# Weighing key rows by attention probabilities in three float32r passes, in a decoder layer on one Trainium2 core

## The reference

```python
q = l @ Wq                                  # l: normed latents (x after the first layer norm)
kv_in = jnp.concatenate([x, l], axis=1)     # normed context and latents: the 128 "key rows" of a batch
k, v = jnp.split(kv_in @ Wkv, 2, axis=-1)
w = jnp.einsum('bhqd,bhkd->bhqk', q * scale, k * scale)
w = jax.nn.softmax(w, axis=-1)
out = jnp.einsum('bhqk,bhkd->bhqd', w, v)
return out.transpose(0, 2, 1, 3).reshape(B, S_lat, INNER) @ Wo
```

## Time and profile before

| | us |
|---|---|
| median of three runs | 1594.77 |
| lowest, highest of them | 1588.36, 1599.34 |
| the profiled execution | 1598.73 |
| its span from first to last instruction | 1596.9 |
| TensorE busy in the span | 1421.5 (89%) |
| VectorE, ScalarE, GpSimd busy | 1102.3, 1033.0, 901.6 |

### The profile page before, as it was taken

One profiled execution on the slowest core, in us unless ns is written; L12 is line 12 of the kernel. 1 busy time (PEld: TensorE's weight loads), 2 busy tenths in 40 slices (PEclk: granted clock), 3 DMA queues, 4 the chain that ended last, 5 costly groups with the idle time before them and its releaser, 6 DMA issues. The chain is left out here.

```text
span 1596.9 us, 36673 instructions
## 1 busy us (share of the span) xinstructions
PE 1421.5 (89%) x10509; PEld 1235.3 (77%) x10509; DVE 1102.3 (69%) x4106; ACT 1033.0 (65%) x3829; POOL 901.6 (56%) x1233
## 2 busy tenths in 40 slices
PE   6799999999999999999999999999995688889940
PEld 4688888888878888888888888888884688889940
DVE  4466677776677777777767777677656577777765
ACT  3577777777777777776777767777762455555535
POOL 4355665666666666566665566656544255545555
PEclk8899999999999999999999999999998899999975
DMA  3000000000000000000000000000001776667746
GB/s 88 11 11 10 16 15 15 17 18 14 17 15 16 18 15 16 15 16 18 15 16 15 17 15 18 16 15 8 10 10 42 222 221 211 216 200 231 206 140 203
DMA packets 64625, 96.19 MB, mean 60 GB/s; under 512 B 10892, under 2 KB 48786, under 8 KB 64306
## 3 DMA queue, kind: packets, MB, share of 16 engines
q1 hardware_dynamic: 44738, 71.90, 15.1%
q0 software_dynamic: 8896, 16.94, 3.1%
q10 hardware_dynamic: 10800, 5.06, 1.2%
HBM read 71.55 MB, written 23.35 MB: 59 GB/s over the span
## 5 line engine op out<-in xcount | busy, mean ns | idle before, releaser
L696 ACT ACTIVATE probs<-ps_s,neg_max 128x128 f32<-128x128 f32 x1024 | 361.7, 366 | 291.2 <-DVE neg_max L929 291.2
L511 POOL TENSOR_TENSOR probs_n<-probs,inv_sum 128x512 f32<-128x512 f32 x256 | 265.9, 1039 | 250.4 <-DVE inv_sum L935 248.4
L1348 PE MATMUL ps_s<-kvT,u_sb 128*128 128x128 f32 x2048 | 281.1, 280 | 0.8 <-issue 0.8
L1348 PEld LDWEIGHTS ps_s<-kvT,u_sb 128*128 128x128 f32 x2048 | 255.2, 192 | 34.2 <-issue 33.1
L1381 PE MATMUL ps_t<-pT,kv_rows 128*128 128x512 f32 x512 | 262.2, 594 | 0.8 <-DVE pT L941 0.8
L1361 PE MATMUL ps_o<-value_w,tT 128*128 128x128 f32 x2048 | 260.7, 275 | 2.6 <-ACT tT L707 2.4
L1361 PEld LDWEIGHTS ps_o<-value_w,tT 128*128 128x128 f32 x2048 | 244.0, 192 | 4.5 <-ACT tT L707 4.5
L929 DVE TENSOR_REDUCE neg_max<-ps_s 128x4 f32<-128x512 f32 x256 | 176.2, 688 | 101.8 <-PE ps_s L1348 101.4
L609 POOL DMA_INDIRECT y_rows<-wvT,f_id x144 | 145.6, 1011 | 160.8 <-DVE wvT L1265 111.2
L696 ACT ACTIVATION_READ_ACCUMULATOR probs<-ps_s,neg_max 128x1 f32 x1024 | 208.1, 203 | 0.0
L523 POOL DMA_INDIRECT x_rows<-routed,pos_i x128 | 136.8, 1069 | 120.4 <-DVE pos_i L1037 99.5
(11 more groups left out here) (268 smaller groups left out, 3164.2 us busy)
## 6 DMA issues: line engine op xcount, KB each, us to landing
u_sb<-in_expert_w SPq DMA_DIRECT2D x45, 578.0 KB
tT<-in_expert_w SPq DMA_DIRECT2D x27, 578.0 KB
f_x<-x_rows SPq DMA_DIRECT2D x72, 130.0 KB
tT<-y_rows SPq DMA_DIRECT2D x16, 512.0 KB, 4.5
x_raw<-in_x SPq DMA_DIRECT2D x64, 64.0 KB, 1.8
c_raw<-in_ctx_in SPq DMA_DIRECT2D x64, 64.0 KB, 2.0
out<-u_sb ACTq DMA_DIRECT2D x16, 256.0 KB, 2.7
y_rows<-wvT,f_id POOLq DMA_INDIRECT x144
```

What stands on the lines that cost most here:

```text
L511: nc.gpsimd.tensor_tensor(probs_n[:, sl], probs[:, sl], inv_sum[:, sl, :].rearrange("p (u o) -> p u o", o=1).to_broadcast([P, UP, P]), ALU ...
L696: last = nc.scalar.activation(probs[:, sl, j], ps_s[sl][:, j * P:(j + 1) * P], ACT.Exp, bias=neg_max[:, sl, j:j + 1], accum_out=sums[:, sl ...
L1348: last = nc.tensor.matmul(ps_s[sl][:, j * P:(j + 1) * P], u_sb[:, c // 2, BT * p + b, h:h + 2].rearrange("p h s -> p (h s)"), kvT[:, c, 2 ...
```

## The change

`kv_rows` and `pT` each become two float32r tiles, `hi` and `lo`, and `weigh` becomes three products. ScalarE's new `round_pT` copies `ps_pT` to `pT_hi`; `keep_pT` on VectorE now waits for that and subtracts, `pT_lo = ps_pT - pT_hi`. ScalarE's `keep_rows` writes `kv_hi`, and a new `rows_low` on VectorE writes `kv_lo`. `turn_probs` waits for `pT_lo_done`. The lists of TensorE, ScalarE and VectorE are reordered; GpSimd's and SyncE's are not.

```diff
-                nc.scalar.activation(kv_rows[:, j % KV_RING], KV_BACK.rearrange("p (b d) -> p b d", b=BT),
-                                     ACT.Copy).then_inc(kv_done, 1)
+                nc.scalar.activation(kv_hi[:, j % KV_RING], KV_BACK.rearrange("p (b d) -> p b d", b=BT),
+                                     ACT.Copy).then_inc(kv_hi_done, 1)
+            def round_pT(t, k):
+                m, ss = t * 4 + (k - 1), (k - 1) % 2
+                act.wait_ge(pT_ps, m + 1)
+                act.wait_ge(t_ps, count(m - 1))
+                nc.scalar.activation(pT_hi[:, ss], ps_pT[:], ACT.Copy).then_inc(pT_hi_done, 1)
...
                     if on(t, 0):
                         exps(t, k)
+                    if pair_on(t, p):
+                        keep_u(4 * t + 8 + k)
                     if k == 0 and unit_on(t, -2):
                         keep_t(t, 0, p)
+                    if unit_on(t, k - 1):
+                        round_pT(t, k)
                     if k == 2 and on(t, 5):
                         keep_qkv(t + 5)
-                    if pair_on(t, p):
-                        keep_u(4 * t + 8 + k)
...
+            def rows_low(j):
+                dve.wait_ge(kv_hi_done, j + 1)
+                nc.vector.tensor_tensor(kv_lo[:, j % KV_RING], KV_BACK.rearrange("p (b d) -> p b d", b=BT),
+                                        kv_hi[:, j % KV_RING].bitcast(F32), ALU.subtract).then_inc(kv_lo_done, 1)
                 def keep_pT(k):
                     m, ss = t * 4 + (k - 1), (k - 1) % 2
-                    dve.wait_ge(pT_ps, m + 1)
-                    dve.wait_ge(t_ps, count(m - 1))
-                    nc.vector.tensor_copy(pT[:, ss], ps_pT[:]).then_inc(pT_done, 1)
+                    dve.wait_ge(pT_hi_done, m + 1)
+                    nc.vector.tensor_tensor(pT_lo[:, ss], ps_pT[:], pT_hi[:, ss].bitcast(F32), ALU.subtract).then_inc(pT_lo_done, 1)
...
-                lo, hi = ((0, 8), (8, 12), (12, 16))[k - 1]
+                lo, hi = ((0, 6), (6, 10), (10, 16))[k - 1]
...
-                pe.wait_ge(pT_done, m)
+                pe.wait_ge(pT_lo_done, m)
...
-                pe.wait_ge(pT_done, m + 1)
-                pe.wait_ge(kv_done, m // 4 + 1)
+                own = m // 4 % KV_RING
+                pe.wait_ge(pT_hi_done, m + 1)
+                pe.wait_ge(kv_lo_done, m // 4 + 1)
                 pe.wait_ge(t_done, m)
-                nc.tensor.matmul(ps_t[:], kv_rows[:, m // 4 % KV_RING, b], pT[:, ss], start=True, stop=True).then_inc(t_ps, 1)
+                nc.tensor.matmul(ps_t[:], kv_hi[:, own, b], pT_hi[:, ss], start=True, stop=False)
+                nc.tensor.matmul(ps_t[:], kv_lo[:, own, b], pT_hi[:, ss], start=False, stop=False)
+                pe.wait_ge(pT_lo_done, m + 1)
+                nc.tensor.matmul(ps_t[:], kv_hi[:, own, b], pT_lo[:, ss], start=False, stop=True).then_inc(t_ps, 1)
```

More of the change, by code:

```diff
@@ L127, in decoder_layer @@
         KV_RING = 4
-        kv_rows = sb("kv_rows", [P, KV_RING, BT, D])
+        kv_hi = sb("kv_hi", [P, KV_RING, BT, D], F32R)
+        kv_lo = sb("kv_lo", [P, KV_RING, BT, D], F32R)
         kvT = sb("kvT", [P, 4, 4, S])
@@ L147, in decoder_layer @@
         probs_n = sb("probs_n", [P, 2, UP, P])
-        pT = sb("pT", [P, 2, UP * P])
+        pT_hi = sb("pT_hi", [P, 2, UP * P], F32R)
+        pT_lo = sb("pT_lo", [P, 2, UP * P], F32R)
         x2T = sb("x2T", [P, 2, P])
@@ L1037, in place_int @@
                     nc.vector.tensor_copy(pos_i[:, p], pos_f[:, p]).then_inc(pos_done, 1)
+                if on(t, 0):
+                    row_max(0)
                 if on(t, 3):
                     split_latents(t + 3)
-                if on(t, 0):
-                    row_max(0)
                 if on(t, -2):
@@ L1057, in period @@
                     inverse_sum(0)
-                if unit_on(t, -1):
-                    keep_pT(0)
                 if on(t, -4):
@@ L1071, in period @@
                     row_max(1)
+                if unit_on(t, -1):
+                    keep_pT(0)
                 if on(t, -3):
@@ L1083, in period @@
                     inverse_sum(1)
+                if on(t, 4):
+                    x1_norm(t + 4)
                 if unit_on(t, 0):
                     keep_pT(1)
-                if on(t, 4):
-                    x1_norm(t + 4)
                 if on(t, 0):
                     row_max(2)
+                if on(t, 2):
+                    rows_low(t + 2)
                 if on(t, -3):
@@ L1093, in period @@
                     inverse_sum(2)
+                if on(t, -4):
+                    place_all()
                 if unit_on(t, 1):
                     keep_pT(2)
-                if on(t, -4):
-                    place_all()
                 if on(t, 0):
@@ L1111, in period @@
                     rot_add(t + 5)
-                if on(t, 0):
-                    inverse_sum(3)
-                if unit_on(t, 2):
-                    keep_pT(3)
                 if on(t, 5):
@@ L1118, in period @@
                     kv_product(t + 5)
+                if on(t, 0):
+                    inverse_sum(3)
                 if on(t, -4):
@@ L1126, in period @@
                     place_int()
+                if unit_on(t, 2):
+                    keep_pT(3)
                 if on(t, 5):
@@ L1189, in _ @@
             scale_queries(3)
+            rows_low(0)
             in_hats(4)
             residual(3)
+            rows_low(1)
             dve.wait_ge(s_gate, 32)
@@ L1428, in turn_rows_back @@
             def turn_rows_back(j):
-                pe.wait_ge(kv_done, min(j, 2))
+                pe.wait_ge(kv_lo_done, min(j, 2))
                 for b in range(BT):
@@ L1440, in period @@
                         score(t, k, c)
-                    if k == 0:
-                        if unit_on(t, -2):
-                            weigh(t, 0, p)
-                        if pair_on(t, p):
-                            latents_part(4 * t + 8)
-                    if k == 2 and pair_on(t, p):
-                        latents_part(4 * t + 8 + 2)
-                    if k and on(t, -1):
+                    if k == 0 and unit_on(t, -2):
+                        weigh(t, 0, p)
+                    if k and pair_on(t, p):
+                        latents_part(4 * t + 8 + k)
+                    if k == 1 and on(t, -1):
                         out_part(t, k, p)
-                    if unit_on(t, k - 1):
+                    if k and unit_on(t, k - 1):
                         turn_probs(t, k)
+                    if k > 1 and on(t, -1):
+                        out_part(t, k, p)
                     if k == 0 and on(t, 4):
@@ L1456, in period @@
                         nc.tensor.matmul(B_GATE, x2T[:, p3], wg_sb[:], start=True, stop=True).then_inc(gate_ps, 1)
+                    if k == 0:
+                        if unit_on(t, -1):
+                            turn_probs(t, 0)
+                        if pair_on(t, p):
+                            latents_part(4 * t + 8)
                     if k == 2 and on(t, -4):
@@ L1461, in period @@
                         pe.wait_ge(logits_done, min(t - 2, NT))
-                        pe.wait_ge(kv_done, min(t + 3, NT))
+                        pe.wait_ge(kv_lo_done, min(t + 3, NT))
                         nc.tensor.matmul(B_RANK, ones[:], seen[:, p], start=True, stop=False)
@@ L1471, in period @@
                         make_qkv(t + 5)
-                    if k:
-                        if k != 2 and pair_on(t, p):
-                            latents_part(4 * t + 8 + k)
-                        if unit_on(t, k - 2):
-                            weigh(t, k, p)
+                    if k and unit_on(t, k - 2):
+                        weigh(t, k, p)
                     if k == 1 and on(t, 5):
```

8 lines of the change are left out of this document (4 added, 4 removed).

## The result

| | before | after |
|---|---|---|
| median of the runs, us | 1591.57 (1588.13 to 1599.34) | 1551.82 (1550.83 to 1554.91) |
| ratio | | 0.975, 95% interval 0.972 to 0.978 |
| the profiled execution, us | 1598.73 | 1550.83 |
| one period, us | 18.23 | 17.51 |
| start of the first expert transpose | 1247.2 | 1205.9 |

The prediction said 1547, between 1507 and 1577, and faster. The kernel is 2.5% faster: 39.8 us in the medians, 47.9 between the two profiled executions.

The account below looks back on a forecast made before the run. TensorE's list was taken as the bound, but for one stall, at 18.235 us a period. 58 x 0.80 = 46 plus 5 gave 51 off 1598.73: 1548, median 1544, rounded up to 1547; range 1507 to 1577.

Parts of the forecast that it names:

- The stall removed: TensorE's once-a-period wait at `turn_queries` for `kv_product` on VectorE goes, saving 0.74 us a period.
- `weigh`: On TensorE, three float32r passes of 0.22 replace a 0.86 float32 product: 0.20 less, four times, 0.80 us a period.
- The new wait: TensorE waits 0.73 us a period at `turn_probs` for `pT_lo`, with `seen_add` on VectorE blocked under GpSimd's `scale`.
- The period: TensorE's list of 16.70 us plus the 0.73 wait gives 17.43 a period, 0.80 less than before.
- The race: Rival: GpSimd's `scale` starts before `route_rows`' last step (1568, chance 0.09) or first step (1585, chance 0.05).
- The sum: Whole kernel: 58 steady periods x 0.80 = 46, plus 5 from `weigh` in six others, together 51 us.
- No block: Rival: `seen_add` on VectorE is not held; wait 0.05 to 0.1, period 16.8, time 1507; chance 0.10.
- Last step: Rival: `scale` starts before `route_rows`' last step; wait at `turn_probs` 1.15, period 17.85, time 1568; chance 0.09.
- Dear passes: Rival: a 512-column float32r pass in `weigh` takes 0.29, so only the stall's gain remains, 1579; chance 0.04.
- ScalarE slower: Rival: ScalarE's longer list delays the first exponentials and makes the kernel slower, 1617 at 1.2 us late; chance 0.05.

Follow-up runs that it names:

- e1: Kernel before with only the key products (`k_pick`, `kv_prod`) moved ahead of the fourth inverse sum and the copy of `pT`; 1549.8 us.
- e2: Changed kernel with `seen_add` moved from behind `z1_sum` to behind `keep_pT(0)`; 1515.5 us.
- e8: Changed kernel with `seen_add` and `route_rows` both moved behind `keep_pT(0)`; 1501.8 us.
- e7: Changed kernel with three one-column reciprocals, read by nothing, added on VectorE ahead of `route_rows`; 1567.6 us.
- e6: Changed kernel with two extra 512-column ScalarE copies, read by nothing, ahead of each period's first exponentials; 1581.8 us.
- e3: Changed kernel with `weigh` as one float32 product of the upper parts, the lower parts still computed; 1579.0 us.
- e4: Changed kernel with the key products moved back behind the fourth inverse sum; 1558.3 us.
- e12: Kernel before plus three passes, `keep_u` right behind the exponentials, `keep_pT` behind the next row maximum, and the change's TensorE list; 1596.6 us.

## Why the prediction was right

**The stall removed.** Right: no pause at `turn_queries`, in the change and in e1. Its price was 0.68 (e1) and not 0.74.

**`weigh`.** The pass was mis-sized: 0.23, not 0.22, so it saves 0.17 and not 0.20 a product. I took the value near half of the float32 record; the measured one lies in the middle of my bounds (0.215 to 0.24).

**The new wait.** Right in place, cause and size. `turn_probs` was due at 6.22 (I said 6.17) and waited 0.73 (0.73). `route_rows` slipped in ahead of `scale`, `seen_add` was held for 0.92 until its end, `row_max(1)` came at 5.51 (5.6), `pT_lo` at 6.12 (6.2), and TensorE went on at 6.95 (6.9). This is what the row of `pos_sel` in a late period was good for the earlier trace rows: a narrow step of the same form, caught in the same collision. The Trainium skill ("SBUF — State Buffer", "Who interferes with whom") states that a VectorE instruction with two SBUF inputs contends with a GpSimd one that reads SBUF, and the trace agrees: 0.15 against 0.92. e2 shows that the block makes the wait: with `seen_add` elsewhere the period falls by 0.64. That it is the block and not one step less in the list shows in the distance from `z1_sum` to the statistics behind it. It is 0.44 in the kernel before, with `seen_add` unblocked between the two (610.28 in the earlier trace rows and the row below), 0.45 in e2 without it (571.73, 572.18), and 1.10 in the change (605.08, 606.18).

```profile
610.72 0.29 DVE L900 BATCH_NORM_STATS2 st_z<-z 128x6 f32<-128x128 f32 x1
```

**The period.** 17.51 where I had 17.43. Three of the four products lie behind the wait, so the dearer pass makes 0.09 of this; the rest cancels.

**The race.** Its chance was put at 14%. It was not either or: of the 55 steady periods five are 0.36 to 0.55 longer. In four of these `route_rows` loses the race (0.46 and more). There VectorE pauses without a cause in the trace, and its last copy is held; in the fifth the pause lies right ahead of `row_max(1)` and costs 0.36 by itself. One of the four:

```profile
534.57 0.29 DVE L1031 COPY routed<-rows 128x256 f32<-128x256 f32 x1 [0.22 <-issue]
534.78 1.01 DVE L1033 COPY routed<-rids 128x2 int32<-128x2 int32 x1
...
534.65 1.11 POOL L513 TENSOR_TENSOR probs_n<-probs,inv_sum 128x512 f32<-128x512 f32 x1
```

**The sum.** I had 58 periods x 0.80 and 5 for the others, 51. Measured from the first scores to the last: 55 steady periods x 0.69 = 37.8 (0.73 each, less the five long ones), the first four 4.9, the last four 0.2, so 42.9. The number of steady periods was three too high, the four first ones, in which nothing is routed and so nothing held, gained more than `weigh` (up to 1.5 each), and the four last ones nearly nothing. Then 1.0 was lost ahead of the first scores and 0.6 behind the last; at the first expert transpose it is 41.3 (1247.2 and 1205.9).

The other 6.7 of the 48.0 between the spans came in the expert tiles, which the change leaves alone and which vary by more than that from one profile to the next. So the 1550.8 of the profiled execution, beside my 1548, is closer than my terms were: the steps gave 41, not 51, and chance gave part of the rest. The median of after, 1551.8, is 7.8 above the 1544 that the sum gave for it.

**The rivals.** "No block" is e2 and e8: I gave it 1507 and a period of 16.8; they have 1515.5 and 1501.8, with 16.87 and 16.75. "Last step" is e7: 17.85 forecast, 17.97 measured. "Dear passes" fell with the 0.23. "ScalarE slower" did not come about; e6 shows how far off it was.

## What to carry to other kernels

Where an engine that is the bound waits once a period, and the change shortens it and takes the wait away, ask who is next in line before counting the gain: here the new wait took 0.73 of the 1.42 that both edits freed, and moving two small steps out of another engine's way was then worth more than the change itself. If a step moves from one engine to another (here the copy of `ps_pT`), look at every list that it now couples: the passes alone made the kernel slower, one more step moved alone made it worse, and only with all of them moved did it gain. A narrow instruction is not cheap by its width: its price is that of the GpSimd instruction which it may have to sit out, so place it where nothing waits behind it.

## What the runs showed of the hardware

- A float32r pass of 512 columns has a pitch of 0.23, one of 256 columns 0.12, a float32 product of 512 columns 0.86. Three passes save a fifth of the float32 product.
- An eight-column bf16 addition on VectorE is held until `scale` on GpSimd ends: 0.92 and, in another place, 0.96 for a product that makes a mask, where 0.15 and 0.16 are the times alone. A copy of two int32 columns from SBUF to SBUF is held too: 1.01 to 1.10 where 0.16 is the time alone.
- The order of start decides to within some hundredths. A copy 0.19 ahead of `scale` (605.01 and 605.20) took its 0.16, and so did one 0.09 ahead (437.38 and 437.47, e7). One that started 0.03 ahead by its row was held for 1.08.
- Not every GpSimd instruction holds VectorE. In the kernel before, `seen_add` took its 0.15 at 610.54 in the midst of a GpSimd instruction on 128 x 2 elements, which took 0.70 from 610.22 on. From what size on an instruction holds was not tried.
- VectorE pauses about every ninth period, with no releaser in the trace; in the change the rows show 0.06 to 0.29 of idle time. The pauses belong to a place in VectorE's list and not to a time: they stand at the same step of periods 18, 27, 36 and 45 in after, e3, e4, e6 and e12, whose periods differ by 0.7 us. In the kernel before a period with a pause is at most 0.09 longer, in the change up to 0.55, where the pause lies on the path and decides the race too. What the pause is stays open; no run took it apart.
- The stretch from the first expert transpose to the end took 333 to 354 us in fourteen profiles, without relation to the edits. TensorE was busy for 258 to 262 us of it in all of them, and the DMA engines moved 202 to 215 GB/s, less where it took longer; so it is waiting that varies. What moves it stays open.
